# Causal mask of the row maxima as four 64x64 products, and routing in 18 steps with one sum for the denominator

## The reference

```python
x = layernorm(x + attention(x))
# attention: scores = Q K^T * scale; where(causal_mask, -1e6, scores); softmax; @ V; @ Wo + bo
# ffn:
xn = (x - mu) / sqrt(var + 1e-05) * gamma + beta
probs = softmax(xn @ Wg.T)
denom = t1v + t2v + 1e-09          # the two largest of probs
combine = [t1v / denom, t2v / denom]
out = sum over experts of gate * (gelu(xn @ W1 + b1) @ W2 + b2)
x = layernorm(x + x + out)
```

## Time and profile before

| | |
|---|---|
| median of 3 runs (range) | 1107.22 us (1107.21 to 1108.87) |
| the profiled execution | 1104.55 us |
| its span in the trace | 1102.5 us |
| busy: PE, DVE, ACT, POOL | 959.9, 816.1, 665.9, 637.5 us |
| attention part in the trace | up to about 707 us |
| mask products, line 1052 | 1536, from 26.6 to 706.2 us |
| line 1285, DVE | 16, median 1971 ns |

### The profile page before, as it was taken

How to read it: one execution, slowest core, us unless ns; L and a number is a source line. 1 busy time by engine, 2 the same in 40 slices (tenths; PEclk the granted TensorE clock), 3 DMA queues, 4 the chain that set the end, 5 groups by cost and what they waited for, 6 DMA issues and landing times.

```text
span 1102.5 us, 29583 instructions
## 1 busy us (share of the span) xinstructions
PE 959.9 (87%) x9185; PEld 635.4 (58%) x9185; DVE 816.1 (74%) x2134; ACT 665.9 (60%) x1338; POOL 637.5 (58%) x951
## 2 busy tenths in 40 slices
PE   3789999999999999999999999869899889998750
PEld 1344454454545545545544455339899879998740
DVE  3777879888888888898898888954454464467744
ACT  1256566676666676666666766636566745556552
POOL 7022434754855756657647557547757556557874
PEclk9899999999999999999999999979999999999985
DMA  7523133243243242332432423343322222265515
GB/s 163 191 79 114 52 105 113 60 139 104 65 129 105 86 123 83 114 118 71 125 116 54 137 92 90 104 144 78 86 69 85 74 74 78 72 215 171 170 50 171
DMA packets 134567, 117.74 MB, mean 107 GB/s; under 512 B 56218, under 2 KB 99777, under 8 KB 134240
## 3 DMA queue, kind: packets, MB, share of 16 engines
q1 hardware_dynamic: 121808, 96.37, 30.0%
q0 software_dynamic: 8704, 17.06, 4.6%
q10 hardware_dynamic: 3904, 2.43, 1.0%
HBM read 65.26 MB, written 53.81 MB: 108 GB/s over the span
## 4 chain that ended last, share of the span: by engine, by line
PE 50%; DVE 20%; issue 10%; DMA 6%; POOL 6%; ACT 3%; SPq 3%; ACTq 1%; DVEq 0%; POOLq 0%
PE ring L1145 9%; PE ring L1129 9%; DVE negmax L1189 9%; PE ps_v L1069 7%; PE ring L1006 6%; PE ring L1037 5%; PE ring L1052 3%; SPq L397 2%; POOL y_d L633 2%; PE ps_m L899 2%; PE ps_m L917 2%; DVE rv L1285 2%; PE ps_m L934 2%; PE ps_m L904 1%; DVE mt L1218 1%
## 5 line engine op out<-in xcount | busy, mean ns | idle before, releaser
L728 ACT ACTIVATE probs<-ring 128x768 f32<-128x768 f32 (+1 forms) x384 | 337.5, 882 | 211.9 <-PE ring L1006 208.3
L1189 DVE TENSOR_REDUCE negmax<-ring 128x2 f32<-128x1024 f32 (+3 forms) x512 | 410.6, 815 | 62.7 <-PE ring L1052 56.3
L598 POOL TENSOR_SCALAR_AFFINE_SELECT probs<-probs 128x512 f32<-128x512 f32 x256 | 163.1, 639 | 287.0 <-ACT probs L728 285.4
L837 ACT ACTIVATE vpad<-ring,b_s 128x128 f32<-128x128 f32 x576 | 164.3, 369 | 104.9 <-PE ring L1129 103.7
L633 POOL DMA_INDIRECT y_d<-vpad,xs x144 | 146.6, 1018 | 109.9 <-DVE vpad L1488 80.5
L1006 PE MATMUL ring<-qarea,kside 64*128 64x512 f32 (+3 forms) x1024 | 177.7, 385 | 28.6 <-DVE negmax L1189 20.0
L1006 PEld LDWEIGHTS ring<-qarea,kside 64*128 64x128 f32 x1024 | 86.6, 185 | 183.1 <-issue 119.4
L1069 PE MATMUL ps_v<-probs,vpad 128*32 128x512 f32 (+3 forms) x2048 | 180.7, 449 | 4.0 <-POOL probs L598 4.0
L1037 PE MATMUL ring<-kside,qarea 64*128 64x256 f32 (+2 forms) x1024 | 165.0, 360 | 17.3 <-DMA qarea<-qk_d 10.4
L1145 PE MATMUL ring<-qarea,vpad 128*128 x1152 | 158.6, 281 | 18.3 <-ACT vpad L837 17.8
L1129 PE MATMUL ring<-vpad,w_t 128*128 128x128 f32 x1152 | 156.2, 279 | 8.9 <-issue 8.5
(11 more groups left out here) (178 smaller groups left out, 1092.5 us busy)
## 6 DMA issues: line engine op xcount, KB each, us to landing
qk_d<-qarea SPq DMA_DIRECT2D x62, 256.0 KB, 2.5
kside<-qk_d SPq DMA_DIRECT2D x96, 128.0 KB, 3.0
qarea<-qk_d SPq DMA_DIRECT2D x90, 128.0 KB
xs<-rows_d SPq DMA_DIRECT2D x144, 66.0 KB, 1.9
probs<-y_d SPq DMA_DIRECT2D x16, 512.0 KB, 4.5
xin<-L_attn_x SPq DMA_DIRECT2D x16, 256.0 KB, 2.9
att_d<-attt SPq DMA_DIRECT2D x128, 32.0 KB
rows<-att_d SPq DMA_DIRECT2D x16, 256.0 KB
```

The lines of the kernel that those rows point to most:

```text
L598: pool.affine_select(out=diag, in_=diag, pattern=[[0, 4], [1, P]], compare_op=ALU.is_ge, fill=0.0, base=0, channel_multiplier=-1).then_inc ...
L728: nc.scalar.activation(of_unit(h // 2, part), ring[:, 2 * part % 3, :, (0, P, P)[part]:S], ACT.Exp, scale=SCALE).then_inc(sem("exp_done"), 1)
L837: ins = nc.scalar.activation(ht[:, n % 4, c, :], ps_a[:, n % 4, c * P:(c + 1) * P], ACT.Gelu_apprx_tanh, bias=b1_s[:, bass.ds(e, 1), c:c + ...
L1189: ins = nc.vector.tensor_reduce(negmax[:, n // 6 % 2, qb, s:s + 2], ring[:, (2 * n + 1) % 3, :, c0:c0 + nk], AX.X, ALU.max, negate=True)
```

## The change

It has two parts. The first rewrites the mask. `diagb` becomes the bare 64x64 unit matrix, and each product now writes only the 64 query partitions that it masks, so a unit has four products in the four quarters of the array: row half by head, column half by query half. Queries 0 to 63 get 128 columns, queries 64 to 127 only the last 64.

The second shortens the routing by two steps. The difference `lg - best` serves for the first choice too (`is_equal` 0, in one instruction with the product), and the second maximum is taken of differences, so it is `d_best` itself. Both exponentials land in one tile `terms` of 10 numbers, the first eight with a bias of log(1e-9), the ninth the second choice's, the tenth a constant 1; their sum is the denominator. The reciprocal and the last product follow one and two places earlier, at `at` 13 and 14.

```diff
-    ROUTE = 20
+    ROUTE = 18
...
-        diagb = sb("diagb", [P, 3 * P // 2], BF16)
+        diagb = sb("diagb", [P, P // 2], BF16)
...
+        terms = sb("terms", [P, QB, E + 2])
+        tiny = sb("tiny", [P, 1])
...
+            pool.memset(terms[:], 1.0)
+            pool.memset(tiny[:], math.log(1e-9))
...
-                        nc.scalar.activation(rt[:, 2], rt[:, 1], ACT.Exp).then_inc(sem("gate_exp"), 1)
+                        nc.scalar.activation(terms[:, :, 0:E], rt[:, 1], ACT.Exp, bias=tiny[:, :]).then_inc(
+                            sem("gate_exp"), 1)
                 if h == 3 and i.plus(-3).exists(NB):
-                    need(act, sem("route"), ROUTE, i.plus(-3), 8)
-                    nc.scalar.activation(rv[:, 4], rv[:, 3], ACT.Exp).then_inc(sem("gate_exp"), 1)
+                    need(act, sem("route"), ROUTE, i.plus(-3), 7)
+                    nc.scalar.activation(terms[:, :, E], rv[:, 3], ACT.Exp).then_inc(sem("gate_exp"), 1)
...
                 for c in range(2):
-                    at = HALF * (1 - c)
+                    queries = slice(HALF * c, HALF * (c + 1))
                     for half in range(2):
                         rows = half_of(half)
-                        to = ring[:, (2 * n + 1) % 3, half, :]
-                        past = pastb[rows, at:at + P]
+                        to = ring[queries, (2 * n + 1) % 3, half, :]
+                        past = pastb[rows, HALF:(3 - c) * HALF]
                         if n % 3 == 2:
-                            to = to.rearrange("p (a n) -> p a n", n=P)[:, 0:QB:QB - 1, :]
-                            past = past.unsqueeze(1).broadcast_to([HALF, 2, P])
+                            to = to.rearrange("p (a n) -> p a n", n=P)[:, 0:QB:QB - 1, c * HALF:P]
+                            past = past.unsqueeze(1).broadcast_to([HALF, 2, P - c * HALF])
                         else:
                             c1 = (QB - 1 - n % 3) * P
-                            to = to[:, c1:c1 + P]
-                        ins = pe.matmul(to, diagb[rows, at:at + P], past, start=False, stop=(c == 1))
+                            to = to[:, c1 + c * HALF:c1 + P]
+                        ins = pe.matmul(to, diagb[rows, :], past, start=False, stop=True)
...
-                lambda b: [V.tensor_tensor(eq1, lg[:], along(best, E), ALU.is_equal),
-                           V.tensor_tensor(diff, lg[:], along(best, E), ALU.subtract)],
-
-                lambda b: [V.tensor_tensor(w1c, eq1, wtab[:], ALU.mult)],
+
+                lambda b: [V.tensor_tensor(diff, lg[:], along(best, E), ALU.subtract)],
+
+                lambda b: [V.scalar_tensor_tensor(out=w1c, in0=diff, scalar=0.0, in1=wtab[:], op0=ALU.is_equal,
+                                                  op1=ALU.mult)],
...
-                lambda b: [V.tensor_reduce(v2, rest, AX.X, ALU.max)],
-                lambda b: [V.tensor_tensor(eq2, rest, along(v2, E), ALU.is_equal),
-                           V.tensor_tensor(d_best, v2, best, ALU.subtract)],
+                lambda b: [V.tensor_reduce(d_best, rest, AX.X, ALU.max)],
+                lambda b: [V.tensor_tensor(eq2, rest, along(d_best, E), ALU.is_equal)],
...
-                lambda b: [V.tensor_reduce(z, ex, AX.X, ALU.add)],
-                lambda b: [V.scalar_tensor_tensor(out=z, in0=z, scalar=1e-9, in1=e2, op0=ALU.mult, op1=ALU.add)],
-                lambda b: [V.tensor_scalar(z, z, 1.0, None, ALU.add)],
+                lambda b: [V.tensor_reduce(z, terms[:, :, :], AX.X, ALU.add)],
                 lambda b: [V.reciprocal(g(b, 0), z)],
...
                 if n == 15:
-                    need(dve, sem("gate_exp"), 2, b, 1)
-                if n == 16:
                     need(dve, sem("gate_exp"), 2, b, 2)
...
-                        if 12 <= at < 17:
+                        if 12 <= at < 15:
                             route(late, 3 + at)
```

More of the change, by code:

```diff
@@ L16 @@
 from contextlib import ExitStack
+import math
 import concourse.bass as bass
@@ L555, in _ @@
             link(pool.memset(lowerb[:], 0.0))
-            mid = diagb[:, HALF:2 * HALF]
-            link(pool.affine_select(out=mid, in_=mid, pattern=[[-1, HALF]], compare_op=ALU.not_equal, fill=1.0,
+            link(pool.affine_select(out=diagb[:], in_=diagb[:], pattern=[[-1, HALF]], compare_op=ALU.not_equal, fill=1.0,
                                     base=0, channel_multiplier=1))
-            pool.affine_select(out=mid, in_=mid, pattern=[[-1, HALF]], compare_op=ALU.not_equal, fill=1.0,
+            pool.affine_select(out=diagb[:], in_=diagb[:], pattern=[[-1, HALF]], compare_op=ALU.not_equal, fill=1.0,
                                base=-HALF, channel_multiplier=1)
@@ L1251, in _ @@
             V = nc.vector
-            best, d_best, z, e2, c1, v2, c2 = (rv[:, k] for k in (0, 3, 6, 4, 1, 2, 5))
-            eq1, diff, ex, w1c, m1, rest, eq2, w2c, m2, place, p1, p2 = (rt[:, k] for k in range(12))
+            best, d_best, z, c1, c2 = (rv[:, k] for k in (0, 3, 6, 1, 5))
+            diff, w1c, m1, rest, eq2, w2c, m2, place, p1, p2 = (rt[:, k] for k in (1, 3, 4, 5, 6, 7, 8, 9, 10, 11))
+            e2 = terms[:, :, E]
             def g(b, k):
@@ L1259, in _ @@
                 lambda b: [V.tensor_reduce(best, lg[:], AX.X, ALU.max)],
[L1261 to L1264 removed]
+                lambda b: [V.tensor_tensor(diff, lg[:], along(best, E), ALU.subtract)],
+                lambda b: [V.scalar_tensor_tensor(out=w1c, in0=diff, scalar=0.0, in1=wtab[:], op0=ALU.is_equal,
+                                                  op1=ALU.mult)],
                 lambda b: [V.tensor_reduce(c1, w1c, AX.X, ALU.max)],
                 lambda b: [V.tensor_tensor(m1, wtab[:], along(c1, E), ALU.is_equal)],
[L1268 removed]
+                lambda b: [V.scalar_tensor_tensor(out=rest, in0=m1, scalar=NEG, in1=diff, op0=ALU.mult,
                                                   op1=ALU.add)],
[L1270 to L1272 removed]
+                lambda b: [V.tensor_reduce(d_best, rest, AX.X, ALU.max)],
+                lambda b: [V.tensor_tensor(eq2, rest, along(d_best, E), ALU.is_equal)],
                 lambda b: [V.tensor_tensor(w2c, eq2, wtab[:], ALU.mult)],
```

1 line of the change is left out of this document (removed).

## The result

The changed kernel takes 1121.70 us (median of 4 runs, 1114.51 to 1123.39), the kernel before 1107.22 in the same session: ratio 1.0107, 95% interval 1.007 to 1.0144. Forecast was 1106.5, within 0.2% of no change. The profiled execution took 1122.04 us with a span of 1120.0, 17.5 us more than the span before.

What follows compares the result with a forecast made beforehand. TensorE bounds: 40.9 us own work a pass plus waits for VectorE. 40.9 + 1.6 + 0.3 = 42.8 against 43.05 gives -3.0 us over twelve passes, +2.4 over three: total -0.6, forecast 1106.5 us, range 1085 to 1124.

Steps and rivals of the forecast that it cites:

- The sign: Whole kernel: 0.6 us faster than the profiled execution, given as 1106.5 us; chances faster 0.42, same 0.19, slower 0.39.
- so I take no stall: DVE routing: product e2 x gate in line 1285's old slot starts about 0.05 us before POOL's select, so does not stall.
- rival (c): DVE routing: product in line 1285's slot still waits for select and gamma product; waits +0.55 us a pass, 1113 us; chance 0.08.
- The mask, +1.6 us of PE work a pass: Attention mask on PE: shape changes and exposed loads outweigh shorter products over 24 units; bounds +0.9 to +3.1 us.
- the five direct ones: Mask units followed directly by scores: the exit becomes a shape change too, +0.19 us each, 0.95 us a pass.
- Rival (b): Mask on PE: 64 x 128 to 64 x 64 is no shape change; much faster, 1078 us; chance 0.17.
- rival (a): Mask on PE: quarters cost +3.1 us a pass, loads and second pairs in the open; 1127 us; chance 0.15.
- The waits, 2.15 to 0.3: Attention passes: PE's waits for DVE fall from 2.15 to 0.3 us a pass, bounds 0 and 1.0.
- What is late next is PE itself: Attention passes: once the waits for DVE fall to 0.3 us a pass, PE itself is the next thing late.
- The stall of line 1264: DVE routing: line 1264, 0.63 us when stalled, comes 0.1 us earlier against POOL's select and no longer waits.
- The price of a shape change at the entry: PE, from line 1037 into the mask: a change of tile shape costs 0.09 us in all 24 units.
- The first three passes: Passes before the twelve: dearer mask, no routing stall, part hidden in DMA and ScalarE waits; +0.8 us each, +2.4 together.

Runs made afterwards that it cites:

- e9: The changed kernel as it is, run again beside e10, e11 and e12 on one chip: 1118.91 us, ratio 1.0110 to the kernel before.
- e3: Changed kernel with the routing's reciprocal moved from slot 13 to 14 and last product from 14 to 16: 1102.12 us, ratio 0.994.
- e5: Changed kernel with POOL's gamma product issued at h = 6 instead of h = 7: 1138.51 us, ratio 1.0001 to the kernel before.
- e2: Routing half alone: the changed kernel with the mask of before: 1101.39 us, ratio 0.9927 to the kernel before.
- e8: Kernel before, with the second mask product of each row half writing only the last 64 columns: 1137.95 us, ratio 0.996.
- e12: e11 with the second mask product of each row half writing only the last 64 columns: 1093.91 us, ratio 0.9885 to the kernel before.
- e4: Changed kernel with the mask of before, reciprocal at slot 14 and last product at 16: 1095.39 us, ratio 0.9866 to the kernel before.
- e6: Changed kernel with all four quarter mask products at full column width (extra columns zeros): 1152.52 us, ratio 1.010 to the kernel before.
- e11: Same kernel as e4, run on the chip of e9: 1097.87 us, ratio 0.9921 to the kernel before.
- e10: Same kernel as e3, run on the chip of e9: 1106.49 us, ratio 0.9982 to the kernel before.
- e1: Mask half alone: the kernel before with the mask part of the change: 1110.98 us, ratio 1.0032 to the kernel before.

## Why the prediction was wrong, point by point

**The sign.** Without falls the forecast of the sum came out: 42.8 us a pass was forecast, and the passes of the changed kernel with the stall and without a fall are 42.94 (two in e9). Ten of these would be 429.4 us, 2.3 less than before, where 2.5 less was forecast; the trace has 444.55, 15 us more for ten falls. With the eleventh fall that makes 17 us; 1121.7 less 17 is 1105, where 1106.5 was forecast. That the sum came out is partly luck, as two of its terms were off in opposite ways (below). The step that failed is one that the prediction never took: it priced every instruction at the clock that the trace of before granted, 1.00, and had no term for what the change does to the clock. That passes with a fall are this much longer is measured. That the falls of the changed kernel need the stall is shown by e3 and e5 (stall away, those falls away), that they need the quarters by e2 (mask of before, one early fall left). That it is the stall's two waits through which it acts is argued: e5 keeps one of them and has no fall, e2 keeps both, longer, and has one. Why the quarters are needed as well, and why of two passes equal to 0.01 us only one falls, no run here tells; the columns were tried and are not it. What stays untried is to give PE other work inside the two waits.

**The stall, "so I take no stall".** Failed, and rival (c), given 0.08, held: the product waited through select and gamma product, 2.07 us. The argument was the row of line 1264, which ended with the first POOL instruction. The prediction named the 0.04 us of start as the margin; the start is no protection at all. The product starts 0.16 before the select, but the indirect DMA of line 616 was still running then, to 0.14 us behind the product's start, and the prediction did not name that row. (c) was priced at +0.55 a pass, 1113; its true price is the 1.5 us fall behind it.

Rows of e8 show both behaviours in one kernel: lines 1264 (0.56 to 0.58 us) and 1285 (1.97). The first ends with the select, though another POOL instruction of one operand follows at once; the second goes on through the gamma product, which has two. The same in e12, where the product of slot 16 takes 0.60 three times and ends with the select. That the kind of the next POOL instruction decides is argued from these rows, not tested; e5 shows only that the stall goes when the row of POOL work is broken up. The Trainium skill (SBUF — State Buffer, Who interferes with whom) says that a VectorE instruction with two SBUF inputs contends with a GpSimd instruction that reads SBUF, and one with a single input does not unless it is in a two-port mode. The reciprocal of 0.17 us against the product of 2.07 in the same place agrees with it. Line 1285 of the kernel before has one input and waited 1.97 us; whether it ran in such a mode no trace shows.

**The mask, +1.6 us of PE work a pass.** Mis-sized: +0.71 (e3 against e4), below even the lower bound of 0.9. The directions were right: an entry costs 0.09 more in 20 of the 24 units (0.04 in the four whose mask stands between 384 columns and the values); the column halves run side by side (e6); the exit to direct scores costs 0.17 instead of 0.10. From start to start, where PE does not wait, e3 against e4 gives 7 x 0.05 + 4 x 0 - 8 x 0.01 + 5 x 0.17 = 1.1 us a pass. So about 0.5 of the 0.9 us by which the term was wrong are prices: 0.05 for each of those four units, which cost nothing, +0.01 for each of the eight of 256 columns, which gain 0.01, and 0.19 for 0.17 in the five direct ones. Behind some of the five PE waits for a maximum, and the dearer exit goes into that wait, which busy time does not count; that may explain the other 0.4, but was not tested. The load takes 104 ns instead of 96. The exits are 0.17 and 0.23, where the prediction's terms without a load give 0.15 and 0.21, so at most 0.02 of it lies in the open, not 0.03. The rule that column tiling switches fast weight load off (the Trainium skill, TensorEngine Tiling (Array Packing), Gotcha 2: Feature Incompatibilities) may hold, but costs 8 ns a load in these rows and at most 0.02 us a unit on PE's path. Rival (b) is refuted by the 0.33, rival (a) by the 0.71 (or 1.1), although (a)'s 1127 stood nearest to the result for another reason.

**The waits, 2.15 to 0.3.** Failed twice over. With the stall 1.6 us stayed. Without it 1.0 stays in e3 and 1.3 to 1.6 in e4, and most of that is for ScalarE and DMA, which the trace of before hardly names, because PE came late enough for them. "What is late next is PE itself" was wrong. This error and that of the mask went opposite ways and left 42.8 right: 41.5 of work and 1.1 of waits, not 42.5 and 0.3.

**What held, and what was overlooked.** The stall of line 1264 went: line 1274 takes 0.17 us in every one of these passes. Its neighbour was not in the prediction: line 1273, the product `eq2 * wtab`, took 0.65 us in the four occurrences where lines 1264 and 1272 did not stall, and 0.17 in the others. Its successor, line 1283, takes 0.62 to 0.65 us in all of its first twelve. So one such stall a pass is left, always the same one, which is how the passes became alike; no wait of PE is put down to it. The price of a shape change at the entry held within 0.01 us in 20 of the 24 units. The first three passes were forecast at +0.8 each, with no routing stall in them, and came out at -1.5 together: line 1264 stalled there too (0.63 us at 167.1), and PE waited 2.5 us in the second and in the third of them and waits 1.0 and 1.1 now, so there was more to give way than I had counted.

## What to carry to other kernels

A sum at the clock of the old trace is good only while the engine's waits keep their places: look where a change leaves waits of half a microsecond, two close together above all, and give a fall of the clock its own rival, here 1.5 us a pass. Before a short two-operand VectorE instruction is put into a slot, read which POOL instructions run at its start and which follow without a gap; a free slot two places on was worth 1.3 to 1.7% with the quarters (and their falls), 0.6% with the mask of before (e2 to e4). And when a wait is taken away, list what the engine would wait for next at an earlier time, since the old trace does not show a resource that was always early.

The best version found keeps the 18-step routing, moves the reciprocal to slot 14 and the last product behind the gamma product, keeps the mask in 64x128 tiles, and drops the 64 columns of zeros: ratios 0.9871 and 0.9885 on two chips. Without the last of these steps it is 0.9866 and 0.9921 (e4, e11). The column saving alone is hardly told apart from none: the intervals of e11 and e12 overlap, and that of e8 against the kernel before ends at 0.9993.

## What the runs showed of the hardware

- The granted clock of a PE that is busy for 96% of a pass (42.86 of 44.47 us) went to half for 3.4 us, after two waits of 0.5 to 0.6 us with 0.8 us of work between them. In one kernel eleven passes in a row did so; in e2, with waits of 0.65 and 0.59 and the mask of before, one of eleven. In e10 single waits of 0.89 and 0.53 us stood ahead of a fall. The Trainium skill (TensorE: Matmul & The Clock Gate, A second HAM failure mode: psum-queue depth-cycling) tells of short idle times between groups of matmuls that make the clock swing; this trace agrees, with 0.59 and 0.54 us and TensorE waiting for PSUM banks to be read, but e2 shows that such idle times do not always do it.
- Two passes with equal rows differed in it (e1), and the same kernel had 11 falls in one profile and 9 in another; its runs spread over 9 us in one session.
- Products in 64x64 tiles in the four quarters of the array: 0.24 us for four of 128 columns, all or half of the columns in one half; the weight load of 64 columns takes 104 ns, of 128 columns 96.
